# Expert networks: output biases as products of split halves, first weight halves taken between, scatters released by the places alone

## The reference

```
xe = layernorm(x)
scores = xe @ router_w + router_b            # [625, 8]
gates  = top-2 of 8 (layer 0: softmax over the two; layer 1: softmax over all, then the two)
out = sum over experts e of gates[:, e] * (h_e(xe) @ w_last[e] + b_last[e])
x = x + out
```

## Time and profile before

| | us |
|---|---|
| Median of 3 runs | 2384.33 (2377.15, 2384.33, 2384.42) |
| Profiled execution, own time | 2380.06 |
| its span | 2378.3 |
| PE busy / PE weight loads / DVE / ACT / POOL | 2108.6 / 2026.9 / 1434.2 / 921.2 / 425.6 |

### The profile page before, as it was taken

The page is one execution under the profiler, slowest core; times in us unless marked ns, Lnnn a source line. Parts: engine busy times, 40 slices in busy tenths (PEclk is TensorE's granted clock), DMA queues, the critical chain, the costliest instruction groups (busy, mean ns, idle before and its releaser), DMA issues. The chain is left out here.

```text
span 2378.3 us, 32233 instructions
## 1 busy us (share of the span) xinstructions
PE 2108.6 (89%) x12766; PEld 2026.9 (85%) x12766; DVE 1434.2 (60%) x2271; ACT 921.2 (39%) x1216; POOL 425.6 (18%) x224
## 2 busy tenths in 40 slices
PE   5997999999999999999879859788878868999994
PEld 5896999998999999999758859687778857999994
DVE  7654456555763233433568863358884676888884
ACT  2342155555341111121137622125512224777772
POOL 1573400000301443533010023111120010000001
PEclk9998999999999999999969979898989977999997
DMA  6112233333340111110269851110112037999995
GB/s 217 42 29 82 74 114 117 114 121 122 136 144 28 60 41 60 40 60 1 64 225 324 280 193 60 47 45 28 63 54 84 11 115 274 362 372 371 382 366 180
DMA packets 158239, 326.89 MB, mean 137 GB/s; under 512 B 14376, under 2 KB 99336, under 8 KB 158090
## 3 DMA queue, kind: packets, MB, share of 16 engines
q1 hardware_dynamic: 133354, 265.66, 31.8%
q10 hardware_dynamic: 18976, 43.31, 5.1%
q0 software_dynamic: 5760, 15.86, 2.2%
HBM read 278.22 MB, written 46.49 MB: 137 GB/s over the span
## 5 line engine op out<-in xcount | busy, mean ns | idle before, releaser
L632 PE MATMUL banks<-weight_hi,xt_hi 128*128 128x384 f32 (+2 forms) x2208 | 739.9, 335 | 60.6 <-DVE xt_lo L1399 14.3
L635 PE MATMUL banks<-weight_lo,xt_hi 128*128 128x384 f32 (+2 forms) x2208 | 724.8, 328 | 0.0
L636 PE MATMUL banks<-weight_hi,xt_lo 128*128 128x384 f32 (+2 forms) x2208 | 724.0, 328 | 0.0
L632 PEld LDWEIGHTS banks<-weight_hi,xt_hi 128*128 128x128 f32 x2208 | 424.8, 192 | 72.2 <-issue 24.2
L635 PEld LDWEIGHTS banks<-weight_lo,xt_hi 128*128 128x128 f32 x2208 | 424.8, 192 | 0.4 <-issue 0.2
L636 PEld LDWEIGHTS banks<-weight_hi,xt_lo 128*128 128x128 f32 x2208 | 424.4, 192 | 0.0
L1861 DVE TENSOR_TENSOR weight_lo<-weight_raw,weight_hi 128x2304 fp32r<-128x2304 f32 (+2 forms) x153 | 341.2, 2243 | 57.7 <-ACT weight_hi L1135 57.2
L1135 ACT ACTIVATE weight_hi<-weight_raw 128x2304 fp32r<-128x2304 f32 (+2 forms) x153 | 287.6, 1883 | 114.1 <-PE banks L632 47.1
L835 POOL TENSOR_TENSOR weight_hi<-weight_raw,columns 128x2304 fp32r<-128x2304 f32 x20 | 80.5, 4027 | 704.2 <-PE banks L632 323.0
L2439 PE MATMUL banks<-held_hi,a_rel 128*128 128x384 f32 (+1 forms) x550 | 170.6, 338 | 3.3 <-ACT a_rel L1078 2.8
L1625 DVE TENSOR_TENSOR held_lo<-banks,held_hi 128x384 fp32r<-128x384 f32 x80 | 44.6, 558 | 213.0 <-ACT held_hi L1063 213.0
(11 more groups left out here) (400 smaller groups left out, 3569.1 us busy)
## 6 DMA issues: line engine op xcount, KB each, us to landing
weight_raw<-L_ffn_w_in SPq DMA_DIRECT2D x102, 1152.0 KB, 7.5
weight_raw<-L_gnn_W_in SPq DMA_DIRECT2D x32, 1152.0 KB, 5.5
weight_raw<-L_ffn_W_in SPq DMA_DIRECT2D x17, 1152.0 KB, 7.6
products<-bias_rows SPq DMA_DIRECT2D x80, 192.0 KB, 1.8
slot_in<-slot_rows ACTq DMA_DIRECT2D x34, 384.0 KB, 5.1
slot_out<-bias_rows ACTq DMA_DIRECT2D x34, 384.0 KB, 6.4
weight_raw<-L_ffn_W_in SPq DMA_DIRECT2D x17, 576.0 KB, 6.5
product_back<-products SPq DMA_DIRECT2D x10, 960.0 KB, 4.7
```

The lines of the kernel that those rows point to most:

```text
L632: ins = pe.matmul(dst, s[0], m[0], start=start, stop=False)
L635: pe.matmul(dst, s[0], m[1], start=False, stop=False)
L636: return pe.matmul(dst, s[1], m[0], start=False, stop=stop)
```

## The change

Three edits, the same for both layers. First, the bias product is made of halves with `mm3`: its operands `combT` and the biases get a hi and a lo, held in a corner of `XT`. ACT makes the three hi (the biases, and the transposed gates in two pieces), after its four weight units; DVE makes the three lo. Thirty fp32r matmuls take the place of ten plain ones. Second, DVE's order is now: lo of unit 0, the three lo of the biases and gates, lo of unit 1, the ten additions, lo of units 2 and 3. Third, POOL's scatters wait for `place` alone.

```diff
-            combT = scoresT
+            flat_XT = [part.rearrange("p k c -> p (k c)") for part in XT]
+            out_b_r = [part[0:EXPERTS, 0:DIM] for part in flat_XT]
+            combT = [part[0:EXPERTS, DIM:DIM + COLS] for part in flat_XT]
...
POOL, expert_rows
-                pool.wait_ge(placed, 2 * (n + 1))
+                pool.wait_ge(placed, 2 * n + 1)
...
ACT, experts
+                def comb_hi():
+                    act.activation(out_b_r[0], out_b[:, :], ACT.Copy).then_inc(combT_ready, 1)
+                    act.wait_ge(comb_full, n + 1)
+                    act.activation(combT[0][:, 0:FULL * P], ps[0:EXPERTS, 5, 0:FULL * P], ACT.Copy).then_inc(combT_ready, 1)
+                    act.activation(combT[0][:, FULL * P:COLS], ps[0:EXPERTS, 6, 0:P], ACT.Copy).then_inc(combT_ready, 1)
                 for _ in range(RING):
                     high()
+                comb_hi()
                 act.wait_ge(sent, 16 * CHOICES * (n + 1))
...
DVE, experts
-                vec.wait_ge(comb_full, n + 1)
-                vec.tensor_copy(combT[:, 0:FULL * P], ps[0:EXPERTS, 5, 0:FULL * P]).then_inc(combT_ready, 1)
-                vec.tensor_copy(combT[:, FULL * P:COLS], ps[0:EXPERTS, 6, 0:P]).then_inc(combT_ready, 1)
-                add_products(PR_FFN[n], X)
...
-                for _ in range(RING):
+                low()
+                vec.wait_ge(combT_ready, 3 * n + 1)
+                vec.tensor_tensor(out_b_r[1], out_b[:, :], f32(out_b_r[0]), ALU.subtract).then_inc(combT_lo, 1)
+                for k, cols in enumerate((slice(0, FULL * P), slice(FULL * P, COLS))):
+                    vec.wait_ge(combT_ready, 3 * n + k + 2)
+                    vec.tensor_tensor(combT[1][:, cols], ps[0:EXPERTS, 5 + k, 0:cols.stop - cols.start], f32(combT[0][:, cols]), ALU.subtract).then_inc(combT_lo, 1)
+                low()
+                add_products(PR_FFN[n], X)
+                for _ in range(RING - 2):
                     low()
                 transposed_lo(0, 0)
...
PE, experts
-                pe.wait_ge(combT_ready, 2 * (n + 1))
+                pe.wait_ge(combT_lo, 3 * (n + 1))
                 for j in range(2 * TILES):
...
-                    pe.matmul(ps[:, (PR_FFN[n] + j) % 8, 0:WCOL], combT[:, t * P:(t + 1) * P], out_b[:, wcols(c)], start=True, stop=True).then_inc(prod_full, 1)
+                    mm3(pe, ps[:, (PR_FFN[n] + j) % 8, 0:WCOL], at(combT, slice(None), slice(t * P, (t + 1) * P)),
+                        at(out_b_r, slice(None), wcols(c)), True, True).then_inc(prod_full, 1)
```

More of the change, by code:

```diff
@@ L437, in build @@
         combT_ready = sem("combT_ready")
+        combT_lo = sem("combT_lo")
         in_b_ready = sem("in_b_ready")
```

## The result

The changed kernel is slower: 2398.31 us median (2394.1 to 2400.47, 6 runs) against 2384.03 (2377.15 to 2384.42, 6 runs), ratio 1.0067 [1.0049, 1.0085]. The forecast was 2375. The kernel was run again later: 2396.52 against 2380.44, 1.0069 [1.0047, 1.0092].

The account below looks back on a forecast made before the run. Taken as bounding: each layer's later chain to the first expert product, bias product and DVE's lo, or scatters and slots. Gains 3.2 + 5.3 = 8.5 us gave 2371.6 or 2375.8; predicted 2375, range 2370 to 2380, with rivals 2366 to 2385.

Parts of the forecast that it names:

- Price of the product: Bias product, both layers: thirty matmuls at 0.32 us, ten products in 9.6 us against 12.8, clock staying at 0.50.
- early release: Scatters waiting for `place` alone, both layers: they and everything behind them start 0.68 us earlier.
- layer 1's second chain: Scatters, load of `slot_in`, transposes, first expert product: transposes at 1974.0 beside early loads, product at 1976.7, gain 5.6 us.
- 2.2 us of slack behind the first chain: Layer 1, before contention: scatters and slots allow the product at 1974.2, bias product and DVE's lo at 1976.4.
- up to 2.5 us late: Layer 1: delay of the scatters' landing from two early weight loads of 1.18 MB, by bytes at 403 GB/s.
- layer 0's: Layer 0's scatters and slots set the start: transposes 1214.3, product 1217.0; with 0.4 us contention 1217.4, gain 3.2 us.
- Hold on POOL: Rival, both layers: DVE's early lo hold POOL's scatters, 3.5 and 6 us late; gain 2 us, 2382; chance 0.06.
- Contention: Early weight loads beside the scatters: up to 2.5 us late in layer 1, 0.4 us allowed in layer 0.
- byte count: Layer 1: 5.1 MB of scatters and weights at 403 GB/s take 12.7 us, all landed by 1970.9.
- The two rivals: DVE's lo hold POOL's scatters (0.06, 2382); loads hold the scatters longer than the bytes say (0.13, 2380).
- Nothing outside the two beginnings changes: Rest of the kernel: no gain or loss counted beyond 3.2 us in layer 0 and 5.3 us in layer 1.
- the shift goes to the end: Layer 1: PE is busy without a gap after the first expert product, so the earlier start reaches the end whole.

Follow-up runs that it names:

- halves_only: The changed kernel with DVE's lo of units 0 and 1 put back behind the ten additions; ratio 0.9988 to the kernel before.
- refills_held: The changed kernel, with SP holding the load of unit 4 and all later ones until the first two slots have landed; ratio 1.0014 to the kernel before.
- code_ahead: The kernel before with ten tiny matmul calls added in each layer while PE waits for the gates; ratio 1.0044 to the kernel before.
- full_turn: The kernel before with 64 tiny calls (256 PE instructions) put ahead of both expert stages; ratio 1.0030 to the kernel before.
- halves_turned: The changed kernel with DVE's lo back behind the additions, new semaphore declared last, 54 tiny calls at the beginning; ratio 1.0023 to the kernel before.

## Why the prediction was wrong

- **Price of the product: right.** Ten products in 9.6 us, 0.32 us a matmul, clock 0.50, PE starting 2.3 us later in layer 1 (worked out: 2.45). halves_only, where PE starts only 0.6 us later, has the remaining 2.6 us in each layer. The early release was right in its start (0.68 us) and worth nothing in its end, since `slot_hot` set that; the 2.46 us in the earlier trace rows said so already.
- **The step that failed: layer 1's second chain** ("2.2 us of slack behind the first chain", "up to 2.5 us late"), and layer 0's with it. It put transposes at 1974.0, 18.6 us behind `gate`; they came at 30.4. Against the 16.7 of before, this is 13.7 us: the last scatter ends 6.7 us later (1981.83 is gate + 18.28, before 11.61), ACT issues its load of the slots 7.2 us behind that end instead of 2.1, 5.1 more, and that load takes 1.9 us more. In layer 0 the transposes are 8.2 us later: 2.1, 2.7 and 3.3.
- **Hold on POOL: given 0.06, and true.** The rival had scatters 3.5 and 6 us late. They were 2.1 and 6.7 late as counted above, though 1.7 of the 6.7 is the lo of unit 2, which the faster product brought beside the last scatter and the rival didn't count. I weighed the wrong row. The earlier trace rows is another scatter beside another, shorter lo, and is unaffected; the earlier trace rows was the very scatter beside a DVE instruction of 2.4 us that reads SBUF alone, and it took 2.5 times its time. The Trainium skill (SBUF — State Buffer, "SBUF: two separate sides") gives the shared ports for a whole instruction to whichever starts first, and has a DVE instruction with two SBUF inputs contend only with a GpSimd instruction that reads SBUF, a condition that the prediction left out. The trace agrees that a scatter waits for the end of such a DVE instruction, but not on the order: the scatter of 1967.41 began first and waited all the same. And every held scatter took 0.84 to 0.95 us more behind DVE's end, in two places beside the next lo. That the ports are the cause isn't shown by any run; the times are.
- **Contention: the byte count is no estimate of it.** I had both ends, nothing and 6.6 us, and took 2.5 to 2.8 in layer 1 and 0.4 in layer 0, as "nearest to the byte count". The loads cost 7.1 and 6.1, on top of the hold., the only row that measured an indirect DMA beside loads, was the better guide. And the sum counted refills 4 and 5 alone; for 6 and 7 it asked whether they were late, not what they would meet. They were 5.4 of the 7.1.
- **The two rivals were one.** The hold moves the scatters back into the refills, and the faster product moves refills 6 and 7 forward into them. Each was priced with the other absent, so no case of mine lay where both hold.
- **"Nothing outside the two beginnings changes", "the shift goes to the end": wrong in layer 1.** The stage has 5 to 7 us more, and in halves_only, where it is 6 to 9 us, this took the halves' 5.2 us as well. Nothing in the profile of before pointed at it that I can name.

In sum: 11.7 us of starts and 7.1 us of stage in the pair of profiles, 18.8 of 20.4; 14.3 us by the medians. Of the starts, shares of the two causes are taken from refills_held; of the stage, that the code's position is enough to do it is shown for the kernel before (code_ahead, full_turn), and for the halves by the stage of one profile (halves_turned), not by the time. That it is all of the 7.1 us in the changed kernel wasn't tried. How a 16 KB packet in one place or another costs a stage its loads is open, and so is whether a fetch that delays PE or one that delays a weight load does it.

## What to carry to other kernels

Before DVE work is moved into idle time, look at what POOL and the DMA queues do in that time, and at what the moved work releases: idle time of one engine is not free when it is another one's issue window. A chain that is to be shortened by a few us is worth only what the next one leaves, so price that one with all mechanisms at once. And where a change adds instructions ahead of a long stage that runs near its load limit, first measure the same number of idle instructions there: here 20 tiny calls were worth 10 us.

## What the runs showed of the hardware that I had not expected

- POOL's indirect DMA, 0.97 us alone, took up to 3.81 us when a DVE subtraction of 128x2304 values out of SBUF (2.55 us) ran beside it, and ended 0.84 to 0.86 us behind DVE, even where it had begun 0.43 us before it.
- Two unneeded loads of 0.79 MB, issued one after the other beside ten scatters, brought their landing from 3.0 to 5.9 us.
- One and the same stage took 370.6 to 373.9 or 383.2 us, by the position of PE's code alone (nothing, 20 or 64 tiny calls ahead of it; a turn is some 250 instructions).
